# Expert layers in tiles of 512 rows with copied weights, and an accumulating scatter into the output

## The reference, cut to what matters

```python
t = x.reshape(-1, orig_shape[-1])          # layer-normed rows, 11776 x 128
gates = jax.nn.softmax(t @ Wr + br, axis=-1)
top_vals, top_idx = jax.lax.top_k(gates, K)             # K = 2
top_vals = top_vals / top_vals.sum(axis=-1, keepdims=True)
for e in range(E):
    h = jax.nn.relu(t @ W1[e] + b1[e])
    y = h @ W2[e] + b2[e]
    out = out + combine[:, e:e + 1] * y
# and the layer's input is added: h = h + ffn(layernorm(h))
```

## Time and profile before

| | us |
|---|---|
| Median of 3 runs | 1806.57 |
| Lowest and highest run | 1805.64, 1807.57 |
| Profiled execution, span from first to last instruction | 1805.6 |
| PE busy, of the span | 1664.1 |
| DVE busy | 1366.9 |
| ACT busy | 1041.9 |
| POOL busy | 766.8 |

### The profile page before, as it was taken

How to read it: one execution, slowest core, us unless ns; L and a number is a source line. 1 busy time by engine, 2 the same in 40 slices (tenths; PEclk the granted TensorE clock), 3 DMA queues, 4 the chain that set the end, 5 groups by cost and what they waited for, 6 DMA issues and landing times.

```text
span 1805.6 us, 42053 instructions
## 1 busy us (share of the span) xinstructions
PE 1664.1 (92%) x10256; PEld 1379.8 (76%) x10257; DVE 1366.9 (76%) x3383; ACT 1041.9 (58%) x2365; POOL 766.8 (42%) x1037
## 2 busy tenths in 40 slices
PE   5999999999999999999799999996999999999940
PEld 4778887888788878887677888875888888888840
DVE  3887888788878888888476777764777777777767
ACT  2777787778777777777464555551333333333334
POOL 1533333233333332333266666674444444444444
PEclk8999999999999999999898999997999999999975
DMA  3222222222222222223655555642111111111149
GB/s 74 80 92 76 83 71 92 75 81 73 92 75 80 75 91 76 79 76 124 214 182 179 210 197 196 220 165 68 51 53 52 52 51 52 51 52 52 50 142 275
DMA packets 149767, 186.51 MB, mean 103 GB/s; under 512 B 15457, under 2 KB 127713, under 8 KB 149602
## 3 DMA queue, kind: packets, MB, share of 16 engines
q1 hardware_dynamic: 120080, 148.93, 24.9%
q0 software_dynamic: 13344, 29.78, 4.9%
q10 hardware_dynamic: 16306, 7.37, 1.4%
HBM read 99.63 MB, written 86.39 MB: 103 GB/s over the span
## 4 chain that ended last, share of the span: by engine, by line
PE 62%; issue 14%; POOL 13%; DVE 5%; DMA 3%; ACT 1%; POOLq 0%; SPq 0%; DVEq 0%; ACTq 0%
POOL sorted_scratch L614 9%; PE bank L1505 7%; PE bank L296 7%; PE bank L1301 6%; PE bank L297 6%; PE bank L298 6%; PE bank L1493 5%; PE bank L1231 4%; PE bank L1329 3%; PE bank L1476 3%; PE bank L1484 3%; PE bank L1508 3%; PE bank L1486 3%; PE bank L1507 3%; PE bank L1485 2%
## 5 line engine op out<-in xcount | busy, mean ns | idle before, releaser
L525 POOL TENSOR_TENSOR prob<-expo,inv 92x368 f32<-92x368 f32 x256 | 205.1, 801 | 517.9 <-DVE inv L974 517.9
L646 POOL DMA_INDIRECT y_scratch<-ytok,goals x192 | 187.9, 979 | 271.1 <-issue 234.1
L863 ACT ACTIVATE hid_h<-bank 128x512 fp32r<-128x512 f32 x192 | 114.9, 598 | 172.8 <-PE bank L1493 172.0
L614 POOL DMA_INDIRECT sorted_scratch<-trow,posi x184 | 179.8, 977 | 56.1 <-issue 55.2
L1505 PE MATMUL bank<-w2s,hid_h 128*128 x768 | 202.5, 340 | 0.5 <-DVE hid_l L1184 0.5
L1301 PE MATMUL bank<-z,xnT 128*92 128x368 f32 x512 | 201.2, 475 | 0.0
L998 DVE TENSOR_TENSOR w2s<-bank,w2s 128x368 fp32r<-128x368 f32 x256 | 136.8, 534 | 69.5 <-ACT w2s L750 69.5
L800 ACT ACTIVATE aT_h<-bank 128x512 fp32r<-128x512 f32 x184 | 110.1, 599 | 133.0 <-PE bank L1364 132.9
L969 DVE TENSOR_REDUCE peak<-bank 92x4 f32<-92x368 f32 x256 | 136.1, 532 | 66.3 <-PE bank L1301 63.3
L1017 DVE TENSOR_TENSOR aT_l<-bank,aT_h 128x512 fp32r<-128x512 f32 x184 | 127.2, 692 | 69.4 <-ACT aT_h L800 61.1
L741 ACT ACTIVATE expo<-cent 92x368 f32<-92x368 f32 x256 | 129.9, 508 | 72.3 <-DVE cent L979 69.8
(11 more groups left out here) (190 smaller groups left out, 4603.2 us busy)
## 6 DMA issues: line engine op xcount, KB each, us to landing
ax_scratch<-val SPq DMA_DIRECT2D x64, 736.0 KB, 3.5
arow<-ax_scratch SPq DMA_DIRECT2D x23, 2048.0 KB, 8.4
tin<-sorted_scratch SPq DMA_DIRECT2D x192, 66.0 KB, 1.8
xin<-in_x_dram SPq DMA_DIRECT2D x32, 372.0 KB
yin<-y_scratch SPq DMA_DIRECT2D x46, 256.0 KB, 4.5
h_scratch<-hT SPq DMA_DIRECT2D x32, 184.0 KB, 4.3
hch<-h_scratch SPq DMA_DIRECT2D x23, 256.0 KB, 8.7
out_dram<-osb ACTq DMA_DIRECT2D x23, 256.0 KB, 4.5
```

The source lines that it names most:

```text
L525: nc.gpsimd.tensor_tensor(prob[:, k % 2], expo[:, k % 2], inv[:, k % 2].unsqueeze(2).to_broadcast([S, HH, S]), ALU.mult).then_inc(prob_kep ...
L614: pool.indirect_dma_start(out=sorted_dram, out_offset=bass.IndirectOffsetOnAxis(ap=posi[:, q, choice, r:r + 1], axis=0), in_=trow[:, q, ch ...
L646: pool.indirect_dma_start(out=y_dram, out_offset=bass.IndirectOffsetOnAxis(ap=goals[:, qm:qm + 1], axis=0), in_=ytok[:, qm % 4], in_offset ...
```

## The change

- Tiles have 512 rows (`TT`); there are `TILES` = 2 * T / 512 + 7 = 53 of them. Tiles past the last filled one take a spare region.
- In a tile, the weights are the stationary operand and 512 tokens stream. So the hidden layer comes out with its width on the partitions, as the second layer wants it, and nothing is turned back. The result of the second layer (`yT`) has the features on the partitions, and four transposes (`turn_y`) turn it to rows.
- The weights of a tile's expert are copied by DMAs of SP inside SBUF, from `w1_h`, `w1_l` and `w2s` to `w1t` and `w2t`, two buffers each. No engine but SP reads the expert's number any more.
- The bias b1 goes into the product. The features of a layer-normed row sum to zero, so feature 127 is replaced by 1, the last row of w1 by b1, and the old last row is subtracted from the other 127. POOL does that in stage one (`w1last` holds the old last row on every partition). The bias b2 is added by ACT when it moves `yT` out of its bank.
- The gates travel with the rows to `sorted_scratch`. DVE weighs the result by them (`weigh_y`).
- Stage two stores the residual rows to `out` (`store_res`) in place of `h1tok`. POOL adds each tile's weighed rows to `out` by 4 indirect DMAs with `compute_op=ALU.add`. All use the semaphore `added`, and the 4 of a tile wait until those of the tile before have landed. `y_scratch` and the loop that read it back are gone. `out` has 512 more rows, which take the results of padding; the caller cuts them off.
- w2 is loaded by 8 DMAs, one for each expert, in place of one.

```diff
-ROOM = T + P
-TILES = 2 * NT + NE
-SPARE = TILES - 2 * NT
...
-RING = 8
...
+TT = 512
+TR = TT // P
+ROOM = T + TT
+TILES = 2 * T // TT + NE - 1
...
+SORTED_ROWS = SPARE_ROW + TT
+OUT_ROWS = T + TT
...
+XRING = 4
+WB = FC * 2 * D
```

```diff
+            def store_res(c, q):
+                at_least(sp, res_kept, c + 1)
+                sl = slice(c * CT, (c + 1) * CT) if isinstance(c, int) else bass.ds(c * CT, CT)
+                sp.dma_start(out[sl, :].rearrange("(r p) d -> p r d", p=P), res[:, q]).then_inc(res_out[q], 16)
+
             def chunk(c, i, q, more):
...
+            def load_w1(n, q):
+
+                e = sp.value_load(whosei[0:1, bass.ds(n, 1)], min_val=0, max_val=NE - 1)
+                at_least(sp, hid_done, FC * (n - 1))
+                for half, src in ((0, w1_h), (1, w1_l)):
+                    sp.dma_start(w1t[:, q % 2, half].bitcast(F32),
+                                 src[:, bass.ds(e * FF, FF)].bitcast(F32)).then_inc(w1_in[q % 2], 16)
+
+            def load_w2(n, q):
+
+                e = sp.value_load(whosei[0:1, bass.ds(n, 1)], min_val=0, max_val=NE - 1)
+                at_least(sp, part_done, FC * (n - 1))
+                sp.dma_start(w2t[:, q % 2].bitcast(F32), w2s[:].rearrange("p e n -> p (e n)")[:, bass.ds(e * WB, WB)].bitcast(F32)
+                             ).then_inc(w2_in[q % 2], 16)
+                at_least(sp, yT_kept, n - 1)
+                sp.dma_start(b2t[:, q % 2:q % 2 + 1], b2T[:, bass.ds(e, 1)]).then_inc(w2_in[q % 2], 16)
+
+            def load_tile(n, q):
+
+                row = sp.value_load(wherei[0:1, bass.ds(n, 1)], min_val=0, max_val=SORTED_ROWS - TT)
+                at_least(sp, added, 16 * TR * (n - XRING + 1))
+                sp.dma_start(tin[:, q], sorted_dram[bass.ds(row, TT), :].rearrange("(p r) w -> p r w", p=P)
+                             ).then_inc(tile_in[q], 16)
+
+            sp.wait_ge(proj_done, AC * NCH)
+            sp.wait_ge(h1_kept, NCH)
+            sp.wait_ge(low_kept, 2 * NE)
+            sp.wait_ge(ws_b2, 16)
             lay_pads(sp, range(0, NE, 2))
             sp.wait_ge(table, 1)
+            for n in (0, 1):
...
+            def tile(n, i, q):
+                if not isinstance(n, int) or n + 2 < TILES:
+                    load_tile(n + 2, (q + 2) % XRING)
+                if not isinstance(n, int) or 2 <= n + 1 < TILES:
+                    load_w2(n + 1, q + 1)
+                if not isinstance(n, int) or n + 2 < TILES:
+                    load_w1(n + 2, q)
+
```

```diff
@@ -550,8 +558,21 @@
                     pool.wait_ge(pair_kept, 2)
                     pool.wait_ge(split_lt, 2)
                     pool.dma_start(raw, w1.rearrange("e d f -> d e f")).then_inc(ws_1, 16)
+                    for half in (0, 1):
+                        pool.dma_start(w1last[half].rearrange("p (e f) -> p e f", e=NE // 2),
+                                       w1[NE // 2 * half:NE // 2 * (half + 1), D - 1, :].partition_broadcast(P)
+                                       ).then_inc(ws_last, 16)
+                    pool.wait_ge(ws_1, 16)
+                    pool.dma_start(raw[D - 1:D, :], b1.rearrange("(o e) f -> o (e f)", o=1)).then_inc(ws_b1, 16)
 
                 if isinstance(g, int) and g == 1:
+                    if k == 0:
+                        pool.wait_ge(ws_b1, 16)
+                        pool.wait_ge(ws_last, 32)
+                    at = slice(k * FF, (k + 1) * FF)
+                    base_at = k % (NE // 2) * FF
+                    nc.gpsimd.tensor_tensor(raw[0:D - 1, at], raw[0:D - 1, at],
+                                            w1last[k // (NE // 2)][0:D - 1, base_at:base_at + FF], ALU.subtract).then_inc(w1_based, 1)
                     low_w(raw[:, k * FF:(k + 1) * FF], w1_h[:, k * FF:(k + 1) * FF], w1_l[:, k * FF:(k + 1) * FF], k)
...
-            pool.dma_start(w2raw[:, :, 1], w2.rearrange("e (c p) d -> p (e c) d", p=P)).then_inc(ws_2, 16)
+            for e in range(NE):
+                pool.dma_start(w2raw[:, e, :, 1], w2[e].rearrange("(c p) d -> p c d", p=P)).then_inc(ws_2, 16)
+            pool.dma_start(b2T[:], b2.rearrange("e d -> d e")).then_inc(ws_b2, 16)
             first_part_over(pool)
```

```diff
+            for half in (0, 1):
+                pool.wait_ge(res_out[half], 16 * ((NCH + 1 - half) // 2))
+            pool.wait_ge(dump_in, 16)
+
             def tile(n, i, q):
-                if is_tile(n):
-
-                    pool_waits((tile_in[q], 16 * (i + 1)),
-                               (y_out[q % 4], 16 * (2 * (i - 1) + q // 4 + 1)))
-                    nc.gpsimd.tensor_copy(goals[:, q:q + 1], tin[:, q, D:D + 1].bitcast(I32)).then_inc(goal_read, 1)
-                m = n - LAG_Y - 1
+                m = n - 1
                 if is_tile(m):
-                    qm = (q - LAG_Y - 1) % RING
-                    pool_waits((goal_read, m + 1),
-                               (y_kept, m + 1))
-                    pool.indirect_dma_start(out=y_dram, out_offset=bass.IndirectOffsetOnAxis(ap=goals[:, qm:qm + 1], axis=0),
-                                            in_=ytok[:, qm % 4], in_offset=None).then_inc(y_out[qm % 4], 16)
+                    b = (q - 1) % XRING
+                    pool_waits((tile_in[b], 16 * ((m // XRING if isinstance(m, int) else i - int(q == 0)) + 1)),
+                               (ytok_kept, m + 1),
+                               (added, 16 * TR * m))
+                    for r in range(TR):
+                        pool.indirect_dma_start(
+                            out=out, out_offset=bass.IndirectOffsetOnAxis(ap=tin[:, b, r, D:D + 1].bitcast(I32), axis=0),
+                            in_=ytok[:, b % 2, r], in_offset=None, compute_op=ALU.add).then_inc(added, 16)
 
```

```diff
-                    act.dma_start(b2s[1:2, :].bitcast(F32), b2_l[:].bitcast(F32)).then_inc(b2_moved, 16)
-
                 if isinstance(g, int) and g == 1:
-                    act.wait_ge(ws_1, 16)
+                    act.wait_ge(w1_based, k + 1)
...
+            def keep_x(n, q):
+                at_least(act, xt_done, n + 1)
+                at_least(act, hid_done, FC * (n - 1))
+                A(x_h[:, q % 2], xt_ps[:], ACT.Copy).then_inc(xh_kept, 1)
+
+            def keep_hid(n, f):
+                at_least(act, hid_done, FC * n + f + 1)
+                at_least(act, part_done, FC * (n - 1) + f + 1)
+                A(hid_h[:, f], hid_ps[f][:], ACT.Relu).then_inc(hidh_kept, 1)
+
+            def keep_yT(m, b):
+                at_least(act, part_done, FC * (m + 1))
+                at_least(act, yt_done, m - 1)
+                A(yT[:, b], y_ps[b][:], ACT.Identity, bias=b2t[:, b:b + 1]).then_inc(yT_kept, 1)
```

```diff
+                at_least(dve, hidh_kept, FC * n + f + 1)
+                V.scalar_tensor_tensor(hid_l[:, f], hid_ps[f][:], 0.0, hid_h[:, f].bitcast(F32),
+                                       ALU.max, ALU.subtract).then_inc(hidl_kept, 1)
+
+            def weigh_y(m, b):
+                at_least(dve, yt_done, m + 1)
+                at_least(dve, added, 16 * TR * (m - 1))
+                V.tensor_tensor(ytok[:, b % 2], yt_ps[:].rearrange("p (r d) -> p r d", r=TR),
+                                tin[:, b, :, D + 1:D + 2].to_broadcast([P, TR, D]), ALU.mult).then_inc(ytok_kept, 1)
+
```

```diff
+            def turn_tile(n, i, q):
+                at_least(pe, tile_in[q % XRING], 16 * (i + q // XRING + 1))
+                at_least(pe, xl_kept, n)
+                for r in range(TR):
+                    ins = nc.tensor.transpose(xt_ps[:, r * P:(r + 1) * P], tin[:, q % XRING, r, 0:D], ident[:])
+                ins.then_inc(xt_done, 1)
+
+            def first_layer(n, i, q, f):
+                b = q % 2
+                if f == 0:
+                    at_least(pe, xl_kept, n + 1)
+                    at_least(pe, w1_in[b], 32 * (2 * i + q // 2 + 1))
+                at_least(pe, hidl_kept, FC * (n - 1) + f + 1)
+                high, low = (w1t[:, b, half, f * P:(f + 1) * P] for half in (0, 1))
+                three(hid_ps[f][:], high, low, x_h[:, b], x_l[:, b], True, True).then_inc(hid_done, 1)
+
+            def second_layer(n, i, q, f):
+                b = q % 2
+                if f == 0:
+                    at_least(pe, yT_kept, n - 1)
+                    at_least(pe, w2_in[b], 32 * (2 * i + q // 2 + 1))
+                at_least(pe, hidl_kept, FC * n + f + 1)
+                high, low = (w2t[:, b, (2 * f + half) * D:(2 * f + half + 1) * D] for half in (0, 1))
+                three(y_ps[b][:], high, low, hid_h[:, f], hid_l[:, f], f == 0, f == FC - 1).then_inc(part_done, 1)
+
+            def turn_y(m, b):
+                at_least(pe, yT_kept, m + 1)
+                at_least(pe, ytok_kept, m)
+                for r in range(TR):
+                    ins = nc.tensor.transpose(yt_ps[:, r * D:(r + 1) * D], yT[:, b, r * P:(r + 1) * P], ident[:])
...
+                    first_layer(n, i, q, 2)
+                if is_tile(n + 1):
+                    turn_tile(n + 1, i, q + 1)
+                if now:
```

(50 more changed lines are left out.)

351 lines of the change are left out of this document (118 added, 233 removed).

## The result

The changed kernel takes 1823.56 us (median of 4 runs, 1819.91 to 1825.06) against 1807.07 (1805.64 to 1808.31) for the kernel before: a ratio of 1.0091 (95% interval 1.0077 to 1.0105). It is slower by 0.9%, and the forecast of 1741 us was wrong. The profiled execution has a span of 1823.3 us, 17.7 more than the 1805.6 before.

A forecast was written before the change was run, and what follows sets the result against it. PE was taken to bound the kernel until the expert loop's end, round trips through `y_scratch` the tail: 1805.6 - 64.2 - 28 (loop) + 1 (larger first tile) + 25 (stage one) = 1740 us span, 1741 median; range 1665 to 1812.

The forecast's parts named there:

- the period: Expert loop: time from tile to tile, forecast at 7.8 + 0.65 + 0.2 = 8.65 us.
- the first tile's scatters: Start of the expert loop: 24 us counted until the first scatters have landed.
- stage one: Stage one: POOL's wait for w1 (7 us) and its new subtraction (18 us) cost +25 us, bounds +3 and +32.
- the tail: After the expert loop: the round trips through `y_scratch` vanish, -64.2 us.
- the price of adding: Expert loop: extra time for adding scatters over writing ones, taken as 1.3 us a tile, at most 3.2.
- d: Expert loop: the unknown extra per tile for adding in place of writing, taken as 1.3 us.
- POOL's chain: Expert loop: a tile's four scatters wait until all before have landed, 6.9 us a tile plus the extra for adding.
- SP's chain: Expert loop: landing, tile load, w2 copy, PE, ACT, DVE, 8.7 us; with the scatters 15.6 + d for two tiles.
- the clock: Expert loop: PE slows after standing still in each tile; 0.2 us a tile, at most 0.7.
- Stage two: Stage two: storing the residual rows costs nothing; 9 us if the prefetch cover went.
- Adding is dear: Rival, expert loop: adding scatters raise the period to 9.9 us or more, slower than before; 14 in 100.

The follow-up runs named there:

- plain_scatter: The changed kernel with output scatters that write instead of adding, all waits kept, sums left out; 1847.32 us, ratio 0.9558 to the kernel before.
- w1_late: The changed kernel with POOL's w1 wait and b1 load moved to the end of group 0, group 1's splits one step later; ratio 0.9979 to the kernel before.

## Why the prediction was wrong

The span was forecast at 1740 and is 1823.3. The 83 us, by my own terms: the period 10.05 for 8.65, 52 * 1.40 = 73 us; the first tile's scatters 2; stage one and the start of the loop 5 (30.7 for 26); the tail 4. That is 84.

**The tail** (-64.2) went, all but 4.4 us: the last scatter starts at 1815.71 and lands, as the others do, 3.2 us later, and the span ends at 1823.3.

**The step that failed: the price of adding.** I took d = 1.3, of it 0.9 for a trip to DRAM and 0.4 for issues. It is 2.75 to 2.8 (3 * 0.6 + 0.95 by the chain). The trip was oversized (what comes after the issue is 0.4 longer), the issues were undersized by far: 0.6 us for each of the four, 2.4 in place of 0.4. My upper bound had issues lengthened by half, 0.48 each, 3.2 us for all of d; it held the measured sum, and I chose a value in its lower half although the operation was not in the trace. The estimate from the Trainium skill's least round trip to HBM ("DMA: Bandwidth & Descriptors", section Latency and other measured facts), 0.8 us as the whole of d, would have been further off still: what the runs show after the issue is about half of that, and what is dear lies on POOL. With d = 2.75 my own working has POOL's chain govern, as it does from d = 1.8: the period is 6.9 + 2.75 = 9.65 us and the time 1741 + 52 * 1.0 = 1793: 52 us of the miss.

**SP's chain was right in kind and 1.5 us short in two tiles**: 10.2 for 8.7. From the landing to PE's product it took 0.4 more, and PE's two groups of three and what stands before the transposes 1.1 more, at half clock. For the clock I had 0.2 us a tile, 0.4 in two. In `plain_scatter`, at the full clock, the same chain is 8.9 us, so most of the 1.5 is the clock, and the clock fell where adding had lengthened the waits: the rest of the price of adding. That keeping PE busy gave back only 0.2 us a tile doesn't clear the term, since POOL's chain took over. By the rows SP's chain gives (10.2 + 9.7) / 2 = 10.0 us; the loop's mean is 10.05, 0.4 us above POOL's 9.65, which makes 21 us. `plain_scatter`, with d = 0, has 8.06 where the formula gives 7.8 + 0.2 = 8.0.

**Two chains nearly equal.** POOL's (9.6) and SP's (10.0) stood so near each other that loosening either gave 0 to 15 us and loosening both 55 us. The forecast's rule that SP's chain is the longer until d = 1.8 was sound for the chain that I had summed; with its measured length SP's stays the longer at d = 2.75 too. In the forecast, too, they stood close: 6.9 + 1.3 = 8.2 and 7.8 + 0.65 = 8.45 us.

**Stage one** was forecast at +25 and came at +29 (up to the first step of group 1 7.2, forecast 7; the eight steps 21.7, forecast 18). Mechanism and place were right, the 7 in part by luck: the changed kernel issues w1 at 51.23, 2.0 us sooner than the kernel before (53.19), for a reason that no run shows, so the wait itself cost 9.2 and `w1_late` gave 9.7 for it. `w1_late` shows that 24 of the 29 were a matter of where the wait and the subtraction stand.

**Stage two** at nothing: right; from the end of stage one to the last sorted rows the shift grows by some 0.3 us only. **The first tile's** scatters have landed 26 us after its first transpose, forecast 24.

**The rivals.** "Adding is dear" is what happened, at its threshold: it needed 9.9 us, and 10.05 it was, but by d = 2.75 and an SP chain lengthened by the clock together, not by d in POOL's chain alone. I had given it 14 in 100.

Some ends in the working are a little off, and none bears on the result: a period of 7.8 gives 1697 and not 1690 us, 9.9 gives 1806 and not 1803, and the sum is 1739.4, which I rounded up.

Whether the waits between tiles could be left out while adding, the runs here don't test; the Trainium skill says of any accumulating DMA that it reads its target and writes it later with nothing held in between, so an overlapping add is lost ("DMA: Bandwidth & Descriptors", section Rules for kernel authors). No run here shows a lost add.

## What to carry to other kernels

A scatter that adds cost twice here: in POOL's issue of each 128 rows, and by turning independent writes into a series in which each group waits for the last one's landing. Before a read-back is replaced by it, multiply both by the number of tiles and set that against the tail, which is paid once (58 us here, at a DMA share of 0.92). A wait that grows can also slow PE behind it: look at the granted clock in the stretch after the wait, not only at its mean. And where one edit gives nothing, look for a second chain of about the same length before dropping the idea: here two edits worth 2 and 15 us alone gave 55 together.

## What was not expected of the hardware

- An adding scatter of 128 rows of 512 bytes holds POOL for 1.55 us, a plain one for 0.96, and has 112 more packets. From the end of the issue it lands only 0.4 us later.
- In the profile a four-byte load for each partition (`b2t`, 0.5 KB) was the last releaser of PE more often than the 512 KB behind which it stood: 30.6 us in 22 waits between 1400 and 1700 us. I can't say whether the load by itself or the copy ahead of it was late; no run tells them apart.
- In one of the two series the kernel before takes 125 us more, and the four kernels traced in it 122 to 125 us more in the second stage. The cause stays open.
